# A node's own softmax term moved from the blend stage into the attention stage, and the low part of y subtracted on GpSimd

## The reference, cut to what matters

```python
src = concatenate([edge_index[0], loops]);  dst = concatenate([edge_index[1], loops])
h = (x @ W).reshape(N, H, C)
e = leaky(a_src[src] + a_dst[dst])
alpha = exp(e - e_max[dst])
denom = segment_sum(alpha, dst)
agg = segment_sum(h[src] * (alpha / denom[dst])[:, :, None], dst)
out = elu(agg + bias + x @ skip_W)
x = layernorm(x + out)
```

## Time and profile before

| what | value |
|---|---|
| median of 3 runs | 6196.12 us (6193.98 to 6201.93) |
| the profiled execution's own time | 6189.36 us |
| its span | 6187.6 us |
| busy over the span | PE 93%, DVE 89%, POOL 77%, ACT 53% |
| attention stage, first message to last add-up | 178 to 2318 us |
| blend stage, first product to last low part | 2330 to 2748 us |
| TensorE's granted clock over the span | 0.981 |

### The profile page before, as it was taken

How to read it: one execution, slowest core, us unless ns; L and a number is a source line. 1 busy time by engine, 2 the same in 40 slices (tenths; PEclk the granted TensorE clock), 3 DMA queues, 4 the chain that set the end, 5 groups by cost and what they waited for, 6 DMA issues and landing times.

```text
span 6187.6 us, 209904 instructions
## 1 busy us (share of the span) xinstructions
PE 5737.5 (93%) x40694; PEld 4573.5 (74%) x40695; DVE 5531.1 (89%) x17615; ACT 3280.7 (53%) x11999; POOL 4743.6 (77%) x4057
## 2 busy tenths in 40 slices
PE   6899999999999997889999999999999999999966
PEld 5555555555555554559999999999999999999944
DVE  2899999999999988989999999999999999999978
ACT  2566666666666654545555555555555555555522
POOL 2777777777777764548888888888888888888878
PEclk8999999999999998889999999999999999999999
DMA  6799999999999984459999999999999999999998
GB/s 198 222 264 263 263 263 263 263 263 264 264 264 263 264 253 152 157 147 178 178 178 178 175 177 176 176 175 175 177 174 177 175 176 174 177 176 174 167 298 294
DMA packets 1269400, 1298.01 MB, mean 210 GB/s; under 512 B 220911, under 2 KB 1180656, under 8 KB 1269264
## 3 DMA queue, kind: packets, MB, share of 16 engines
q0 software_dynamic: 328176, 468.28, 46.3%
q1 hardware_dynamic: 941186, 829.31, 45.6%
HBM read 695.20 MB, written 601.74 MB: 210 GB/s over the span
## 4 chain that ended last, share of the span: by engine, by line
PE 30%; DMA 14%; issue 9%; POOL 5%; DVE 2%; POOLq 1%; ACT 0%; SPq 0%; DVEq 0%; ACTq 0%
DMA part<-arena,c_idx 14%; PE PS L964 8%; PE PS L946 7%; PE PS L935 5%; PE PS L979 5%; PE PS L962 4%; POOL part L584 1%; POOL arena L565 1%; POOL arena L561 1%; POOL d_n L602 1%; POOL out L596 0%; PE PS L954 0%; DVE arena L1302 0%; ACT arena L753 0%; DVE arena L1299 0%
## 5 line engine op out<-in xcount | busy, mean ns | idle before, releaser
L584 POOL DMA_INDIRECT part<-arena,c_idx x1664 | 2615.1, 1572 | 538.3 <-issue 349.3
L545 POOL DMA_INDIRECT big<-h_tab,big x1664 | 1631.4, 980 | 511.7 <-issue 385.6
L860 PE MATMUL PS<-big 128*128 128x260 f32 x3328 | 953.2, 409 | 162.5 <-DVE big L1154 158.2
L964 PE MATMUL PS<-w2m,arena 128*128 128x128 f32 x6656 | 1103.8, 288 | 0.0
L946 PE MATMUL PS<-arena 128*128 128x256 f32 x3328 | 863.1, 382 | 27.9 <-ACT arena L753 26.7
L1162 DVE TENSOR_TENSOR big<-big,PS 128x260 f32 x1664 | 703.2, 423 | 207.9 <-PE PS L860 150.7
L964 PEld LDWEIGHTS PS<-w2m,arena 128*128 128x128 f32 x6656 | 876.9, 192 | 0.0
L860 PEld LDWEIGHTS PS<-big 128*128 128x128 f32 x3328 | 563.7, 189 | 422.6 <-issue 343.9
L659 ACT ACTIVATE big<-PS,arena 128x128 f32<-128x128 f32 x1664 | 513.6, 359 | 667.1 <-PE PS L850 667.1
L752 ACT COPY arena<-PS 128x512 f32<-128x512 f32 x832 | 488.7, 587 | 524.1 <-DMA part<-arena,c_idx 469.0
L729 ACT COPY arena<-PS 128x384 f32<-128x384 f32 x1664 | 718.6, 486 | 31.0 <-PE PS L935 2.8
(11 more groups left out here) (180 smaller groups left out, 10924.2 us busy)
## 6 DMA issues: line engine op xcount, KB each, us to landing
w_tab<-big SPq DMA_DIRECT2D x416, 520.0 KB
arena<-w_tab SPq DMA_DIRECT2D x1664, 130.0 KB
part<-arena SPq DMA_DIRECT2D x1664, 32.1 KB
ot_tab<-big SPq DMA_DIRECT2D x416, 128.0 KB
arena<-ot_tab SPq DMA_DIRECT2D x416, 128.0 KB
arena<-src_tab SPq DMA_DIRECT2D x416, 128.0 KB
arena<-part SPq DMA_DIRECT2D x392, 128.5 KB, 3.5
big<-h_tab,big POOLq DMA_INDIRECT x1664
```

The costliest lines, as they stand in the source:

```text
L545: pool.indirect_dma_start(hg[:, s, k, :], None, h_tab, bass.IndirectOffsetOnAxis(ap=sidx[:, s, k:k + 1], axis=0)).then_inc(s_hg[s], 16)
L584: pool.indirect_dma_start(part[q], bass.IndirectOffsetOnAxis(ap=c_idx[:, s, k:k + 1], axis=0), o_cmb[:, s, k, :], None, compute_op=ALU.add ...
L860: mm(PS[:, 2 + k % 2, 0:HW], oh[:, p, k, :], hg[:, p, k, :], start=True, stop=True).then_inc(s_agg, 1)
L964: last = mm(o_v[:, k, 2 * j:2 * j + 2, :].rearrange("p j u -> p (j u)"), midT[:, k, 1 + j, :], w2m[:, (1 + 2 * j) * MUL:(3 + 2 * j) * MUL] ...
```

## The change

In the attention stage SP loads, once in four groups, one block's rows of h from `h_tab` into a buffer `own_h`. At the end of slot 2 ScalarE multiplies them with `pself`, one instruction to a head. In slot 3 VectorE adds them to the block's rows of `acc`, ahead of that step's first add-up, which now waits for this add. 98 of the 104 turns of four groups do so, and the loop is split in two for it.

In the blend stage the load of h and GpSimd's two operations are gone. VectorE multiplies `acc` itself with `rden`. The subtraction for the low part of y goes to GpSimd, which has it ahead of the power of its step; the buffer of the rests, `b_r`, has four slots instead of two. VectorE's small operation on the variance moves behind the subtraction for the rest of y, and the wait on the load of x moves to the elu. PSUM banks get names.

```diff
             step(i * TURN + slot, slot, lambda v: True)
     for g in range(last, n + tail):
         step(g, g % TURN, lambda v: 0 <= v < n)
+
+
+def steps_with_blocks(eng, n, blocks, lead, tail, step):
+
+    first, last = 2 * TURN, (n - lead) // TURN * TURN
+    assert first <= blocks * TURN <= last
+    for g in range(-lead, first):
+        step(g, g % TURN, lambda v: 0 <= v < n, g // TURN if g >= 0 else None)
+    with eng.Fori(first // TURN, blocks) as i:
+        for slot in range(TURN):
+            step(i * TURN + slot, slot, lambda v: True, i)
+    with eng.Fori(blocks, last // TURN) as i:
+        for slot in range(TURN):
+            step(i * TURN + slot, slot, lambda v: True, None)
+    for g in range(last, n + tail):
+        step(g, g % TURN, lambda v: 0 <= v < n, None)
 
 
...
@@ -394,8 +412,14 @@
             sp.wait_ge(s_hst[1], 16 * (NCH // 2))
             sp.wait_ge(s_sdp, NQ)
 
-            def step_a(g, s, there):
+            hb = h_tab.rearrange("(b p) d -> b p d", p=P)
+
+            def step_a(g, s, there, own):
                 e = (s + 3) % TURN
+                if s == 0 and own is not None:
+                    wait(sp, s_own, own)
+                    sp.dma_start(own_h[:, :], hb[ds(own, 1), :, 0:D].rearrange("o p d -> (o p) d")
+                                 ).then_inc(s_ownin, 16)
                 if there(g + 3):
                     wait(sp, s_f1, g)
                     sp.dma_start(eat[0:2 * NBAS, e, :], one(ea8, g + 3)).then_inc(s_ea[e], 16)
...
                 if there(b + 3):
-                    wait(sp, s_bv, b)
-                    wait(sp, s_bs, b)
+                    wait(sp, s_belu, b)
                     wait(sp, s_bskip, b)
-                    sp.dma_start(b_h[:, n, :], hb[ds(b + 3, 1), :, 0:D].rearrange("o p d -> (o p) d")
-                                 ).then_inc(s_bin[n], 16)
                     sp.dma_start(b_x[:, n, :], one(xb, b + 3)).then_inc(s_bin[n], 16)
                     sp.dma_start(b_xT[:, n, :, :], xv[:, :, ds((b + 3) * P, P)]).then_inc(s_bin[n], 16)
                 m = (s - 3) % TURN
...
-            pool.wait_ge(s_self, 1)
-
             def step_b(b, s, there):
-                n = (s + 2) % TURN
-                if there(b + 2):
-                    hs = b_h[:, n, :]
-                    hs4 = hs.rearrange("p (h c) -> p h c", h=H)
-
-                    wait_apart(pool, s_bin[n], landed(b + 2, n, 3))
-                    g.tensor_tensor(hs4, hs4, pself[:, ds(b + 2, 1), :].rearrange("p o (h c) -> p (o h) c", c=1
-                                                                                  ).to_broadcast([P, H, C]),
-                                    ALU.mult).then_inc(s_bt, 1)
-                    wait_apart(pool, s_bt, 2 * (b + 2) + 1)
-                    g.tensor_tensor(hs, hs, acc[:, ds(b + 2, 1), 0:D].rearrange("p o d -> p (o d)"), ALU.add
-                                    ).then_inc(s_bt, 1)
+                n = (s - 3) % TURN
+                if there(b - 3):
+                    wait(pool, s_bmid, b - 2)
+                    g.tensor_tensor(y3[:, ds(b - 3, 1), 2, :].rearrange("p o d -> p (o d)"), b_r[:, n, :],
+                                    y3[:, ds(b - 3, 1), 1, :].rearrange("p o d -> p (o d)"), ALU.subtract).then_inc(s_blo, 1)
                 if there(b):
                     wait(pool, s_bmv, 3 * (b + 1))
                     g.tensor_tensor(mv[:, s, 3:4], mv[:, s, 2:3], half[:, 0:1], ALU.pow).then_inc(s_brstd, 1)
 
-            steps(pool, NB, 2, 0, step_b)
+            steps(pool, NB, 0, 3, step_b)
 
 
             pool.wait_ge(s_zero, 16 * GROUP * NG)
...
@@ -687,8 +700,14 @@
                     wait(act, s_otst[n], landed(g - 3, n) if there(g - 3) else 0)
                     wait(act, s_ad, g - 2)
                     a.copy(ots[:, n, :, :], otp).then_inc(s_ots, 1)
-
-            steps(act, NG, 3, 3, step_a)
+                if s == 2 and own is not None:
+                    wait(act, s_ownin, own * 16 + 16)
+                    for h in range(H):
+                        last = a.mul(own_h[:, h * C:(h + 1) * C], own_h[:, h * C:(h + 1) * C],
+                                     pself[:, ds(own, 1), h:h + 1].rearrange("p o h -> p (o h)"))
+                    last.then_inc(s_ownp, 1)
+
+            steps_with_blocks(act, NG, NB, 3, 3, step_a)
 
 
             def step_b(b, s, there):
...
                     wait(dve, s_z, 5 * g - 4)
                     v.tensor_tensor(za[:, m % 2, :, :], hg[:, m, :, D:HW], ad[:, m % 2, :, 0:H], ALU.add).then_inc(s_z, 1)
+                if s == 3 and own is not None:
+                    wait(dve, s_ownp, own + 1)
+                    wait(dve, s_acc, GROUP * (g - 2))
+                    x = acc[:, ds(own, 1), 0:D].rearrange("p o d -> p (o d)")
+                    v.tensor_tensor(x, x, own_h[:, :], ALU.add).then_inc(s_own, 1)
+                    wait(dve, s_own, own + 1)
                 if there(g - 2):
                     add_up(0)
                 if there(g - 1):
...
@@ -1239,19 +1265,20 @@
             def step_b(b, s, there):
                 n, m = (s + 1) % TURN, (s - 1) % TURN
                 if there(b + 1):
-                    hs4 = b_h[:, n, :].rearrange("p (h c) -> p h c", h=H)
-                    wait_apart(dve, s_bt, 2 * (b + 2))
-                    v.tensor_tensor(hs4, hs4, rden[:, ds(b + 1, 1), :].rearrange("p o (h c) -> p (o h) c", c=1
-                                                                                 ).to_broadcast([P, H, C]),
+                    v.tensor_tensor(b_v[:, n, :].rearrange("p (h c) -> p h c", h=H),
+                                    acc[:, ds(b + 1, 1), 0:D].rearrange("p o (h c) -> p (o h) c", h=H),
+                                    rden[:, ds(b + 1, 1), :].rearrange("p o (h c) -> p (o h) c", c=1
+                                                                       ).to_broadcast([P, H, C]),
                                     ALU.mult).then_inc(s_bsum, 1)
                 if there(b):
                     wait(dve, s_be, b + 1)
+                    wait(dve, s_bin[s], landed(b, s, 2))
                     v.scalar_tensor_tensor(b_e[:, s, :], b_e[:, s, :], -1.0, b_x[:, s, :], ALU.add, ALU.add
                                            ).then_inc(s_belu, 1)
                 if there(b + 1):
                     wait(dve, s_bsum, b + 2)
                     wait(dve, s_bskip, b + 2)
-                    v.tensor_tensor(b_v[:, n, :], b_h[:, n, :], PS[:, n % 2, 0:D], ALU.add).then_inc(s_bv, 1)
+                    v.tensor_tensor(b_v[:, n, :], b_v[:, n, :], PS[:, SKIP_BANK[n % 2], 0:D], ALU.add).then_inc(s_bv, 1)
                 if there(b):
                     wait(dve, s_belu, b + 1)
                     v.scalar_tensor_tensor(b_v[:, s, :], b_v[:, s, :], 0.0, b_e[:, s, :], ALU.max, ALU.add
...
                     mean_and_variance(s, b, s_bmv)
-                    variance_plus_eps(s, b, s_bmv)
-                if there(b - 3):
-                    wait(dve, s_bmid, b - 2)
-                    v.tensor_tensor(y3[:, ds(b - 3, 1), 2, :].rearrange("p o d -> p (o d)"), b_r[:, (s + 1) % 2, :],
-                                    y3[:, ds(b - 3, 1), 1, :].rearrange("p o d -> p (o d)"), ALU.subtract).then_inc(s_blo, 1)
                 if there(b - 2):
-                    maps = PS[:, 3 + s % 2, :].rearrange("p (j m u) -> p j m u", j=2, m=2)
+                    maps = PS[:, MAP_BANK[s % 2], :].rearrange("p (j m u) -> p j m u", j=2, m=2)
                     wait(dve, s_bout, b - 1)
-                    v.tensor_tensor(b_r[:, s % 2, :].rearrange("p (j u) -> p j u", j=2), maps[:, :, 0, :],
+                    wait(dve, s_blo, b - 5)
+                    v.tensor_tensor(b_r[:, (s - 2) % TURN, :].rearrange("p (j u) -> p j u", j=2), maps[:, :, 0, :],
                                     y3[:, ds(b - 2, 1), 0, :].rearrange("p o (j u) -> p (o j) u", j=2), ALU.subtract
                                     ).then_inc(s_br, 1)
-
-            steps(dve, NB, 1, 3, step_b)
+                if there(b):
+                    variance_plus_eps(s, b, s_bmv)
+
+            steps(dve, NB, 1, 2, step_b)
 
 
             def step_c(u, s, there):
```

## The result

Both kernels, 8 runs each: 6193.98 us before (6182.69 to 6201.93) and 6230.11 us after (6210.66 to 6237.07). The ratio is 1.0056, 95% interval [1.0043, 1.0069]: slower by 36 us where 18 us had been forecast; the time is within the predicted range and 16 us above the predicted one. The profiled execution of the changed kernel took 6237.07 us, 47.7 us more than the profiled one of before.

| stretch of the profiled execution | before | after | difference | predicted |
|---|---|---|---|---|
| attention, first message to last add-up | 2140.1 | 2246.8 | +106.7 | +75 |
| last add-up to last low part (blend) | 429.9 | 368.7 | -61.2 | -57 |
| everything else | | | +2 | 0 |

The account below looks back on a forecast made before the run. Bounds: a VectorE-TensorE ring without slack in the attention stage, VectorE in the blend stage. 6189.4 + 75 - 56 - 1 = 6207, with the median 6.8 us above the profiled run 6214 us; range 6198 to 6234, with all rivals 6165 to 6245.

Parts of the forecast that it names:

- The ring: Attention stage: VectorE's messages and add-ups and TensorE's sums wait for each other without slack, 5.14 us a group.
- 0.77 us longer, 98 x 0.77 = 75 us.: Attention stage: VectorE's new add waits for ScalarE's multiplies, making each group that has it 0.77 us longer, 75 us in all.
- the upper bound of 99: Attention stage: if the four multiplies cost as much as L659 at full width, 1.17 us, 1.01 late, 99 us.
- Lower bound: the multiplies finish in time ... 27 us.: Attention stage: with the multiplies ready, the add alone makes the fourth add-up 0.28 us late, 27 us in all.
- The ScalarE time itself costs nothing.: Attention stage: the four multiplies' 0.93 us lie in ScalarE's idle 1.60 us; without that cover, another 91 us.
- The load costs nothing either.: Attention stage: the 128 KB load, issued two groups ahead, adds 0.5 us of DMA work per four groups and stays hidden.
- Step 4.155 to 3.58 ... 56 us saved.: Blend stage: VectorE's work falls to 3.3 us, TensorE's 3.42 us loop becomes the bound; 97 steps save 56 us.
- the half of 0.55 us: Blend stage: VectorE keeps half its 0.55 us a block of GpSimd interference, with one GpSimd operation instead of two.
- The third rival, TensorE's clock.: Blend stage: at a 3.45 us step TensorE is over 90% busy, its clock might stay up; 72 us saved, 6199; chance 0.14.
- the own term didn't hide: Rival, attention stage: multiplies are done when VectorE's add is reached, costing 27 us, not 75; 6166 us; chance 0.16.
- the subtraction didn't block: Rival, blend stage: GpSimd's subtraction blocks VectorE, which stays the bound at 3.82 us; 32 us saved, 6238; chance 0.14.
- the load was hidden: Rival said otherwise: attention stage's DMA engines at 93% are the limit, the load adds 49 us; 6263 us; chance 0.04.

Follow-up runs that it names:

- Experiment 3: Changed kernel with ScalarE's four multiplies at the end of slot 1 instead of slot 2, VectorE's add left in place; 6157.71 us, ratio 0.9942.
- experiment 4: Changed kernel with ScalarE's multiplies in slot 1 and VectorE's add moved up right behind its third message multiply; 6132.02 us, ratio 0.9905.
- experiment 2: Changed kernel without the attention stage's four multiplies and add; the load of h stays but nothing reads it; 6117.38 us, ratio 0.9885.
- experiment 5: Changed kernel with the low part's subtraction put back from GpSimd on VectorE; 6959.78 us in a slower batch, ratio 1.006 to the kernel before.
- experiment 6: Kernel before with only the low part's subtraction moved to GpSimd; 6934.44 us in a slower batch, ratio 1.0036 to the kernel before.
- experiment 7: Changed kernel with VectorE's small operation on the variance back in its old place; 6980.62 us in a slower batch, ratio 1.0086 to the kernel before.
- experiment 8: Kernel of experiment 4 with TensorE's transposes ahead of the blend stage's skip products; 6917.26 us in a slower batch, ratio 1.0004 to the kernel before.
- experiment 1: Changed kernel without the load, four multiplies and add in the attention stage; 6110.8 us, ratio 0.9873 to the kernel before.

## Why the prediction came out as it did

**The ring.** Right. The other groups take 5.13 to 5.20 us, and what comes late to VectorE's add delays TensorE's third and fourth sum and the next messages one for one. The wait that the prediction named, L1208 on ScalarE's multiplies, is there.

**"0.77 us longer, 98 x 0.77 = 75 us."** The mechanism was right and the size too small: 1.09 us and 107 us, beyond the upper bound of 99. This is the term that was mis-sized. In the group shown, counted from the messages (1203.41 in the earlier trace rows, 1203.53 after), the multiplies start 0.12 us later than taken, since the copy ahead of them, L702, is that much later too. They take 1.10 us instead of 0.93: 378 ns each in the median and 0.24 apart, where I took 0.30 and 0.21 by making L659's figures smaller for width. The release is 0.06 quicker than the 0.22 taken. The first add-up then starts 0.32 us behind the add's end, not 0.22. In sum 0.12 + 0.17 - 0.06 + 0.10 = 0.33 us, by which all four add-ups are later than predicted: the whole of the miss. The row nearest by kind should have stood unshrunk, as in the bound. The Trainium skill, page "ScalarE: Activation LUTs", section "What ACT_TABLE_LOAD costs", gave 1.05 us for the four, an estimate that lies closer to the measured 1.10 than mine, though the 332 ns that it gives for one stand against 378.

**"Lower bound: the multiplies finish in time ... 27 us."** Experiment 3 made just this case: 0.37 us a turn, 36 to 38 us, about the 0.28 taken and the same 0.10 for the first add-up's later start. So of the 107 us some 70 are the multiplies' lateness and 37 the add's place. All but 10 us could be had back (experiment 4).

**"The ScalarE time itself costs nothing."** Right: 1.10 us more in each fourth slot left the group of experiment 3 at 5.14.

**"The load costs nothing either."** Right for this kernel, but by luck. No engine waited for it or for `in_ea` there, most likely because the own-term groups gave the transfers 1.1 us more a turn. Without that delay the stage was 12.7 us longer with the load than without it (experiment 2), and in experiment 4 what is left of the own term is 10.5 us. The fault was to weigh the bytes alone: what was late then was another load on SP's queue.

**"Step 4.155 to 3.58 ... 56 us saved."** Right, with 3.539 and 61 us, but partly for other reasons. TensorE's loop is the bound, as said. The gain comes from GpSimd's two operations being gone (experiments 5 to 7). Once they are, neither the 0.34 us of L1274 nor the place of L1233 matters to the step (experiments 5 and 7), and neither does the half of 0.55 us that I left in. Of that half nothing was left at L1276 and L1284. The subtraction now runs mostly beside other operations. What is prolonged is the short half of L1262, over 0.6 us in 23 of 98 steps: for one 0.66 us from 2555.68 on, just behind the start of L576 (2555.59, 0.70 us), and it ended 0.05 us after it. The Trainium skill, page "SBUF — State Buffer", section "SBUF: two separate sides", says that of a GpSimd and a VectorE operation that need the port pair they share, the first holds it for its whole instruction and the other is blocked. These rows agree with that.

**The third rival, TensorE's clock.** Half right: the granted clock stays at 1.00, the 2.4 GHz level, from 2500 to 2700, and is at 1.2 GHz only in the stage's first stretch; that is worth some 7 us. But the step didn't fall to 3.45, since TensorE's own loop takes 3.42 to 3.64, and TensorE is busy 84 of 100 us and not over 90. The saving was 61 and not 72 us.

**The sum.** -61 against -57 and +107 against +75, so +48 in the profiled pair and +36 in the medians, where +18 was said. No rival took place as it was put: the own term didn't hide, the subtraction didn't block, and the load was hidden. That the time still lies in the range is partly luck: the profiled difference on top of the median of before, 6194 + 48 = 6242 us, is beyond its upper end of 6234, and it is the spread between executions that keeps the median 12 us below that.

## What to carry to other kernels

Where two engines form a ring without slack, a new producer and consumer pair is cheap only where each stands so early in its queue that nothing waits for it. Here the same five instructions cost 107 us at one place, 38 with the multiplies a slot earlier and 10 with the add moved up as well. Price a new chain by the durations of the nearest rows as they are, and count the release behind every dependent instruction. An operation moved off an engine is worth something only while that engine bounds the stage, so redo the bound after the other edits before adding up gains.

## What the runs showed of the hardware that I had not expected

- The attention stage in the form of before takes 2140 us in one batch of runs and 2865 in another (experiment 6), with 196 GB/s instead of 263 in 1200 to 1400 us and a granted clock of 0.93 instead of 1.00. The blend stage of the changed kernel, at 149 GB/s, has the same step in both. Chip number 2 stands in the record at a fast batch and at a slow one, so it stays open what made the gathers and loads slower.
- A GpSimd operation of 0.67 us alone lasts up to 0.93 us beside VectorE's (experiment 6), so the disturbance goes both ways.
- TensorE's granted clock was 1.00 from 3220 to 3420 us in experiment 8, with TensorE busy 155.8 of 200 us and its longest idle times 0.85 us, and 0.91 from 2500 to 2600 before, with 82.1 of 100 us busy and idle times up to 0.70. What made it fall in the second wasn't tried.
- Stages that no edit touches differed from one profile to the next: from the first to the last partial sum of the second layer 3125 us before, 3122 after, 3098 in experiment 1, 3100 in experiment 2 and 3115 in experiment 4. That is why stages were compared and not spans. The cause wasn't looked for.
